# Seven full-precision matmuls of a fused two-layer MoE kernel, each cut into four of 32 output columns

## What is computed

```python
def _L1_ffn_ref(x, U1, V1, b1, U2, V2, b2):      # x: 4096 tokens x 128
    P = jnp.einsum('bsd,dr->bsr', x, U1)         # rank 32
    H = jax.nn.gelu(jnp.einsum('bsr,rf->bsf', P, V1) + b1)   # 512 hidden
    Q = jnp.einsum('bsf,fr->bsr', H, U2)         # back to rank 32
    return jnp.einsum('bsr,rd->bsd', Q, V2) + b2
```

## Time and profile before

| | |
|---|---|
| median of 3 runs | 868.09 us (867.88 to 868.23) |
| profiled execution | 870.64 us |
| its span, first to last instruction | 868.8 us |
| TensorE busy | 861.0 us (99%) |
| VectorE busy | 674.7 us (78%) |
| ScalarE busy | 568.9 us (65%) |
| GpSimd busy | 405.8 us (47%) |

### The profile page before, as it was taken

How to read it: one execution, slowest core, us unless ns; L and a number is a source line. 1 busy time by engine, 2 the same in 40 slices (tenths; PEclk the granted TensorE clock), 3 DMA queues, 4 the chain that set the end, 5 groups by cost and what they waited for, 6 DMA issues and landing times.

```text
span 868.8 us, 12489 instructions
## 1 busy us (share of the span) xinstructions
PE 861.0 (99%) x3797; PEld 690.6 (79%) x3797; DVE 674.7 (78%) x1101; ACT 568.9 (65%) x1026; POOL 405.8 (47%) x376
## 2 busy tenths in 40 slices
PE   9989999999999999999999999999999999999998
PEld 6778888787888888888888888888888887777774
DVE  7856877879689687686686687677666689998988
ACT  7778888765555455555555555555556668889896
POOL 7447784134356352252353343243234427664553
PEclk9999999999999999999999999999999999999999
DMA  9688991023113112012012012011010049591701
GB/s 321 217 257 261 274 271 54 1 88 137 50 49 125 38 49 85 1 49 85 1 49 85 1 50 76 10 49 46 4 49 1 1 82 199 132 195 49 176 14 36
DMA packets 36787, 80.72 MB, mean 93 GB/s; under 512 B 4976, under 2 KB 15216, under 8 KB 34928
## 3 DMA queue, kind: packets, MB, share of 16 engines
q1 hardware_dynamic: 36288, 79.66, 30.7%
q10 hardware_dynamic: 432, 0.26, 0.1%
HBM read 69.03 MB, written 6.57 MB: 87 GB/s over the span
## 4 chain that ended last, share of the span: by engine, by line
PE 88%; POOL 3%; DVE 2%; issue 2%; DMA 2%; ACT 1%; SPq 1%; ACTq 0%; DVEq 0%; POOLq 0%
PE ps L980 18%; PE ps L999 18%; PE ps L985 18%; PE ps L1035 9%; PE ps L1042 9%; PE ps L1040 9%; PE ps L1022 3%; PE ps L1020 3%; DMA GWU<-expert_up 1%; PE ps L1015 1%; SPq L821 1%; DVE Hf L1714 1%; POOL GWU L1759 1%; PE ps L955 1%; DVE HL L1729 1%
## 5 line engine op out<-in xcount | busy, mean ns | idle before, releaser
L1162 ACT ACTIVATE Sg<-ps 128x512 f32<-128x512 f32 x288 | 172.1, 598 | 237.3 <-PE ps L999 236.5
L1704 DVE TENSOR_TENSOR Hf<-ps,Sg 128x512 f32<-128x512 f32 x288 | 197.9, 687 | 139.7 <-ACT Sg L1162 88.0
L1844 POOL TENSOR_TENSOR HL<-Hf,HH 128x512 fp32r<-128x512 f32 x133 | 179.5, 1358 | 169.3 <-ACT HH L1049 159.5
L1049 ACT ACTIVATE HH<-Hf 128x512 fp32r<-128x512 f32 x343 | 214.4, 625 | 15.7 <-DVE Hf L1704 8.4
L1729 DVE TENSOR_TENSOR HL<-Hf,HH 128x512 fp32r<-128x512 f32 x241 | 211.5, 878 | 2.5 <-ACT HH L1049 1.6
L980 PE MATMUL ps<-XHL,WBH 128*128 128x512 f32 x512 | 202.8, 396 | 0.1
L999 PE MATMUL ps<-XHL,WBH 128*128 128x512 f32 x512 | 202.1, 395 | 0.0
L985 PE MATMUL ps<-XHL,WBL 128*128 128x512 f32 x512 | 201.6, 394 | 0.0
L1859 POOL TENSOR_TENSOR XT<-XT,TMP 128x512 f32<-128x512 f32 x64 | 83.5, 1305 | 222.3 <-DVE TMP L1551 222.1
L980 PEld LDWEIGHTS ps<-XHL,WBH 128*128 128x128 f32 x512 | 96.1, 188 | 23.1 <-DVE Hf L1704 1.0
L999 PEld LDWEIGHTS ps<-XHL,WBH 128*128 128x128 f32 x512 | 96.2, 188 | 22.4
(11 more groups left out here) (292 smaller groups left out, 1312.3 us busy)
## 6 DMA issues: line engine op xcount, KB each, us to landing
CWB<-scratch SPq DMA_DIRECT2D x14, 1024.0 KB, 4.6
GWU<-expert_up SPq DMA_DIRECT2D x20, 514.0 KB, 4.4
GWD<-expert_down SPq DMA_DIRECT2D x20, 513.0 KB, 4.9
CWB<-scratch SPq DMA_DIRECT2D x40, 256.0 KB, 5.7
ST<-in_wb_dram SPq DMA_DIRECT2D x8, 768.0 KB, 6.1
ST<-scratch SPq DMA_DIRECT2D x24, 256.0 KB, 8.5
GX<-XT SPq DMA_DIRECT2D x66, 64.0 KB, 3.3
XT<-in_x_dram SPq DMA_DIRECT2D x8, 256.0 KB, 5.4
```

What stands on the lines that cost most here:

```text
L1049: e.activation(HH[:, it.n % NH, 0:it.cols], hidden_place(it), ACT.Copy).then_inc(s_hi_act, 1)
L1162: e.activation(Sg[:, it.n % NG, :], z_place(z)[:, :], ACT.Silu).then_inc(s_act, 1)
L1704: e.tensor_tensor(Hf[:, it.n % NS, :], z_place(z)[:, :], Sg[:, it.n % NG, :], ALU.mult).then_inc(s_prod, 1)
L1844: e.tensor_tensor(HL[:, it.n % NH, :], Hf[:, it.n % NS, :], HH[:, it.n % NH, :].bitcast(F32), ALU.subtract).then_inc(s_lo_pool, 1)
```

## The change

In a whole item, the one product with 128 output columns becomes four products in a row. Number q takes columns 32q to 32q + 31 of the item's 128 weight columns as its stationary operand and writes partitions 32q to 32q + 31 of the bank. All four read the same moving tile Hf. `start` and `stop` are set as before on each of them, and the signal is on the fourth. The waits stand before the first, as they did. Nothing else in the kernel differs.

```diff
                 if it.whole:
                     e.wait_ge(s_u2, 5)
                     e.wait_ge(*hidden(it))
-                    e.matmul(bk[:, :], U2F[:, it.f * P:it.f * P + P], Hf[:, it.n % NS, :], start=it.new,
-                             stop=it.last).then_inc(s_down, 1)
+                    for q in range(4):
+                        c = it.f * P + 32 * q
+                        mm = e.matmul(bk[32 * q:32 * q + 32, :], U2F[:, c:c + 32], Hf[:, it.n % NS, :], start=it.new,
+                                      stop=it.last)
+                    mm.then_inc(s_down, 1)
                     return
```

## The result

| | before | changed |
|---|---|---|
| median, 12 runs each | 868.16 us (866.98 to 869.93) | 869.99 us (868.39 to 871.11) |
| profiled execution | 870.64 us | 870.37 us |
| its span | 868.8 us | 868.5 us |
| matmul rows | 3797 | 3839 |

The ratio is 1.0020 (95% interval 1.0012 to 1.0027), so the change costs 1.0 to 2.3 us: slower, as forecast, but by a sixth of the +11.8 us, and a little outside the range (870.6 to 889). The number alone can't tell the prediction's cases apart: 870.0 us also lies in the range of its rival "not slower" (868.1 to 870.1), next to "side by side" (871.5). Nor do the spans of the two profiled executions help, which differ by 0.3 us in the other direction. What decides is the time of an item, stage by stage in the two traces.

What follows compares the result with a forecast made beforehand. TensorE was taken as the bound. Each item takes 2.24 + 0.30 = 2.54 us in place of 0.86, +1.68; seven items give +11.8 us on 868.09, so 879.9 us, range 870.6 to 889.

Steps and rivals of the forecast that it cites:

- not slower: Rival, chance 0.08: quarters overlap and changing form costs next to nothing; at most +0.28 us an item, 868.1 to 870.1 us.
- side by side: Rival, chance 0.30: each quarter has its own line; 1.35 us an item, +0.49 each, +3.4 in all, 871.5 us.
- all seven items count: Five last-stage items (+8.4 us) and two early ones (+3.4 us) all delay the TensorE chain.
- Counted in full: The two early items, at 751 and 791 us, move all that follows, adding their whole +3.4 us.
- two passes of 0.43 us: At the changed line, each narrow float32 product still needs two passes: eight an item, 0.43 us each.
- change of form: Going from 128-column products to 32-column ones and back around each item: 0.30 us an item, lower end 0.09.
- program order, 2.24 us: Likeliest case, chance 0.38: an item's passes start strictly in order across quarters, 2.24 us an item, 879.9 us in all.
- five steps for eight passes: Each quarter's second pass holds back the next quarter, giving 5 x 0.43 + 3 x 0.03 = 2.24 us an item.
- 0.38 against 0.30: Chances given to passes in program order (879.9 us) and to quarters running side by side (871.5 us).
- low end: Bottom of the range: quarters side by side with only the five late items counted, +2.5 us, 870.6 us.
- two bare loads an item: Uncovered weight loads in two steps of each item, 0.10 us more for each.
- likeliest case alone: Narrower span for passes in program order: 876.4 us (five items) to 881.5 us (with bare loads).

Runs made afterwards that it cites:

- 28 items: All four items of blocks 0 to 6 made whole in both kernels: kernel before, wide products, 875.11 us; changed kernel, quarters, 884.93 us.

## Why the prediction was wrong, point by point

- *TensorE is the bound, and all seven items count.* Right. 28 items showed 0.35 us each, nearly the 0.33 of the chain, and the shift of the two traces grows at both early items. "Counted in full" was slightly off: 0.31 us was given back before the last stage, at least 0.16 of it where a product had been waiting for HL before, a wait that the earlier trace rows can't show. The prediction did not look at what TensorE's weight loads waited for (3.1 us for GpSimd's HL between 793 and 856 us).
- *A narrow float32 product has two passes of 0.43 us.* Right: 56 rows, and 0.44 us a pass, with a part of the change of form, where all go to one quarter.
- *The change of form costs 0.30 us an item.* Right: 0.31 us with one narrow product, 0.33 with four, 0.35 with two of 64 columns, paid once when the set is doubled. That it came this close is in part luck, since it was read at one place of the trace, with operands of only 4 and 8 moving columns, and 0.10 us of it there was the bare load of the wide product behind, which is bare here as well.
- *How eight passes share the array: program order, 2.24 us.* This step failed: the five steps for eight passes, 2.24 us. The runs showed two steps in their place, four passes at a time: eight passes took 0.99 us on the chain, 0.13 more than two wide ones, and three more quarters cost 0.03 us. A product on another quarter does not wait for the second pass of the product ahead of it. The prediction took the order of the rows as evidence for strict order, but all of these use the same columns of the array, where even independent quarters would run in order. The rows could not tell the two cases apart, and nothing in the trace stood behind the weight of 0.38 against 0.30. The Trainium skill, "TensorE: Matmul & The Clock Gate", Part 3, says two things here. Its rule of some 4 ns a column tile was the useful one: the estimate by it in the prediction was 870.3 us, and a tile measured some 10 ns (0.03 us for three). Its sentence that matmuls start in strict program order does not hold here if the passes reach TensorE product by product, which is the likely order but not a proven one: the first pass of quarter 3 starts about 0.4 us before the second pass of quarter 0.
- *The price of the side-by-side rival, 1.35 us an item.* Too high by 0.16, which makes 7 x 0.16 = 1.1 of the 1.5 us between that rival's 871.5 and the median. The 0.031 us an instruction pair was read from products that all reload one quarter; on four quarters the eight loads take 0.16 us together and four passes start within 0.04 us. With 1.19 us an item the rival gives 868.1 + 2.3 = 870.4 us, and with what was given back before and in the last stage (0.3 and 0.1 us) 870.0, the measured median.
- *The range* began at 870.6 because its low end used the 0.49 us an item of that rival with the early items at nothing. With the parts as measured the same rule would give 5 x 0.33 = 1.65 us, 869.7. The last stage was to grow by 8.4 us and grew by 1.54. A slip in the sums without weight: two bare loads an item make 7 x 0.20 = 1.4 us, so the likeliest case alone ended at 881.3 and not at 881.5.

## What to carry to other kernels

Before a case is priced from the order of instructions in a trace, ask whether the rows could have come out otherwise; products on the same part of the array say nothing about whether other parts are independent. Cutting a wide float32 product into quarters gains nothing by itself: the passes overlap almost fully, and each excursion from the 128-column form and back costs 0.3 us. Quarters pay where each does different work, as four products in 1.2 us in place of 2.2 to 2.6, and only as long as TensorE stays the bound behind it.

## What the runs showed of the hardware

- Float32 products on different 32-column quarters run side by side though each has two passes: with the products in the order of quarters 0, 1, 2, 3, the first passes of all quarters start within 0.04 us and the second ones about 0.45 us later. On one quarter the same eight take 3.55 us. That each quarter has a line of its own explains this; that the passes are handed over in the order q0, q0, q1, q1, ... is inferred.
- Leaving the 128-column form for 32 or 64 columns and coming back costs 0.31 to 0.35 us around products of 512 moving columns, whatever the number of narrow products between (1, 2, 4 or 8).
- Four quarters with four different moving tiles take as long as with one (1.06 us from first start to last end).
- Weight loads of 32 columns to different quarters overlap: eight loads of 108 ns in 0.16 us.
